# Attention probabilities are split by query rows and turned by DMA; scores run seven units ahead, heads load by fives

## The reference

```python
q = heads(hidden_states @ W_q); k_t = heads(text_ehs @ W_k); v_t = heads(text_ehs @ W_v)
probs_t = softmax(einsum('bhsd,bhtd->bhst', q, k_t) * Dh ** -0.5)
text_out = einsum('bhst,bhtd->bhsd', probs_t, v_t)
attn_scores = einsum('bhsd,bhnd->bhsn', q, heads(ip_ehs @ W_k_ip)) * Dh ** -0.5
qsem = l2norm(einsum('bhst,bte->bhse', probs_t, text_ehs))
sem = einsum('bhse,bne->bhsn', qsem, l2norm(ip_ehs))
probs_ip = softmax(attn_scores + 0.5 * sem) * spatial_mask
out = (text_out + probs_ip @ v_ip) @ W_out + b_out + residual
```

## Time and profile before

| what | us |
|---|---|
| median of three runs | 1904.91 |
| lowest and highest | 1904.19, 1909.89 |
| the profiled execution | 1911.86 |
| its span | 1910.1 |
| PE busy in the span | 1878.8 |
| DVE busy | 1460.1 |
| ACT busy | 1378.5 |
| POOL busy | 907.3 |

### The profile page before, as it was taken

One profiled execution on the slowest core, in us unless ns is written; L12 is line 12 of the kernel. 1 busy time (PEld: TensorE's weight loads), 2 busy tenths in 40 slices (PEclk: granted clock), 3 DMA queues, 4 the chain that ended last, 5 costly groups with the idle time before them and its releaser, 6 DMA issues.

```text
span 1910.1 us, 52608 instructions
## 1 busy us (share of the span) xinstructions
PE 1878.8 (98%) x15701; PEld 1275.4 (67%) x15701; DVE 1460.1 (76%) x3192; ACT 1378.5 (72%) x2644; POOL 907.3 (47%) x1076
## 2 busy tenths in 40 slices
PE   5999999999999999999999999999999999999999
PEld 3776667666666666666666666666666666666555
DVE  5454544788888888888888888888888888888885
ACT  3344554788888888888888888888888888888611
POOL 2121222455555555555555555555555555555421
PEclk8899999999999999999999999999999999999999
DMA  5345555111111111111111111111111111111023
GB/s 174 105 133 130 165 141 140 40 26 27 45 26 27 27 43 26 27 41 29 26 27 45 26 27 27 43 26 27 27 43 27 27 26 44 28 27 51 1 86 107
DMA packets 120643, 102.10 MB, mean 53 GB/s; under 512 B 53369, under 2 KB 114433, under 8 KB 120609
## 3 DMA queue, kind: packets, MB, share of 16 engines
q1 hardware_dynamic: 118304, 99.50, 19.3%
q10 hardware_dynamic: 2304, 2.14, 0.4%
HBM read 67.21 MB, written 34.39 MB: 53 GB/s over the span
## 4 chain that ended last, share of the span: by engine, by line
PE 96%; DVE 2%; ACT 1%; issue 0%; DMA 0%; SPq 0%; ACTq 0%; DVEq 0%
PE bank L1291 29%; PE bank L1292 18%; PE bank L1272 15%; PE bank L1157 13%; PE bank L1265 7%; PE bank L1297 3%; PE bank L1358 3%; PE bank L1290 3%; PE bank L1216 1%; PE bank L1359 1%; DVE reduced L894 1%; DMA reduced<-in_ctx 0%; PE bank L1343 0%; PE bank L1140 0%; ACT u_sb L688 0%
## 5 line engine op out<-in xcount | busy, mean ns | idle before, releaser
L509 POOL TENSOR_TENSOR weight<-probs,half_hi 128x508 f32<-128x508 f32 x640 | 736.1, 1150 | 649.4 <-DVE discard L973 640.1
L1291 PE MATMUL bank<-u_sb,probs_hi 127*128 127x508 f16 x2560 | 943.4, 375 | 0.0
L1292 PE MATMUL bank<-u_sb,probs_hi 127*128 127x508 f16 (+3 forms) x2560 | 760.8, 297 | 0.0
L966 DVE TENSOR_REDUCE neg_max<-bank 128x1 f32<-128x508 f32 x640 | 439.4, 687 | 239.1 <-PE bank L1265 239.1
L712 ACT ACTIVATE probs_hi<-bank 127x512 f16<-127x512 f32 x640 | 382.1, 597 | 234.8 <-PE bank L1272 234.8
L1290 PE MATMUL bank<-v_ring,probs_hi 127*128 127x41 f16 x2560 | 468.5, 183 | 0.0
L978 DVE SCALAR_TENSOR_TENSOR probs_lo<-bank,probs_hi 127x512 f16<-127x512 f32 x640 | 438.8, 686 | 2.4 <-ACT probs_hi L712 2.4
L701 ACT ACTIVATE probs<-bank,neg_max 128x508 f32<-128x508 f32 x640 | 434.3, 679 | 0.5 <-DVE neg_max L966 0.4
L973 DVE SCALAR_TENSOR_TENSOR discard<-bank,weight 128x508 f32<-128x508 f32 x640 | 433.4, 677 | 1.1 <-PE bank L1292 1.1
L708 ACT ACTIVATE half_hi<-probs 128x508 f16<-128x508 f32 x640 | 401.4, 627 | 20.4
L1290 PEld LDWEIGHTS bank<-v_ring,probs_hi 127*128 127x128 f16 x2560 | 248.0, 97 | 226.2 <-issue 0.8
(11 more groups left out here) (160 smaller groups left out, 1340.1 us busy)
## 6 DMA issues: line engine op xcount, KB each, us to landing
x_sb<-in_x SPq DMA_DIRECT2D x16, 640.0 KB, 5.4
reduced<-in_ctx SPq DMA_DIRECT2D x32, 256.0 KB, 5.1
q_ring<-q_parts SPq DMA_DIRECT2D x160, 48.0 KB
k_ring<-k_parts SPq DMA_DIRECT2D x160, 47.6 KB
u_parts<-u_sb SPq DMA_DIRECT2D x8, 825.5 KB, 4.2
u_sb<-u_parts SPq DMA_DIRECT2D x8, 825.5 KB, 4.7
v_parts<-v_sb SPq DMA_DIRECT2D x8, 820.0 KB, 8.0
v_ring<-v_parts SPq DMA_DIRECT2D x160, 41.0 KB
```

The costliest lines, as they stand in the source:

```text
L509: nc.gpsimd.tensor_tensor(weight[:, st % 2, :], probs[:, st, :], half_hi[:, st % 2, :], ALU.subtract)\
L966: nc.vector.tensor_reduce(neg_max[:, st:st + 1], bank[S_BANK + st % 2][:, 0:T], AX.X, ALU.max, negate=True)\
L1291: nc.tensor.matmul(y, hi_k, u_sb[0:TP, par, GH[k]:GH[k] + T], start=(k == 0), stop=False)
L1292: last = nc.tensor.matmul(y[:, k * TP:T], hi_k, u_sb[0:TP, par, UL[k]:UL[k] + U_COLS[k]], start=False, stop=(k == TT - 1))
```

## The change

- The four PE transposes, probs_lo from the bank, half_hi and weight are gone. ACT now shifts the exponential by a constant (an extra instruction on 128 x 1 that makes exp_bias out of neg_max) so that its result is already in the scale of the halves. ACT rounds probs to f16 in query rows (hi, into the tile flat, which lies over the weights' tile wkv). lo is probs minus hi, also in query rows: DVE makes it for 5 units of 8, POOL for units 1, 4 and 6 of 8. POOL adds lo to probs in place (weigh), and the norm takes that sum.
- One DMA transpose on SP turns both halves of two units, 128 x 2048 f16 (turn), into a ring of eight units (turned, over the tile late). flat holds four units.
- The scores have four banks and run seven units ahead (LEAD). probs is a ring of ten.
- Loads come for five heads at once into two buffers (load_group and load_values, seven DMAs). ACT starts them, in step 9 of 20, and the Gram matrix of the next batch but one too.
- The copy of the v bank stands in ACT's even steps j, for the pair that ends with unit j-9 (DRAIN_AT).
- In the first stage all stores are finished before the first loads of the loop are started. The columns of W_q, W_k and W_k_ip come in another order, for which a mask is made by sixteen chained selects at the start, and the image-prompt scores take all 80 columns for each tile.
- Several tiles now lie over others; the image-prompt matrices of the last stage are made earlier.

```diff
@@ sizes, rings and banks
-    RING = 4
...
+    GROUP = 5
+    ROUND = 2 * GROUP * ST
+    ROUNDS = UNITS // ROUND
+    LEAD = 7
+    PROB_RING, FLAT_RING, TURNED_RING = 10, 4, 8
+    POOL_LO = (1, 4, 6)
...
-        S_BANK, PT_BANK, Y_BANK, O_BANK = 0, 2, 4, 6
+        S_BANK, Y_BANK, O_BANK = 0, 4, 6
+        S_BANKS = 4
...
+        def need(eng, signal, count):
+            if not isinstance(count, int) or count > 0:
+                eng.wait_ge(signal, count)
...
+        def load_group(eng, b, i, n):
+            heads = bass.ds(i * GROUP, GROUP)
+            for a0, copies in ((0, 3), (3, 2), (5, 1)):
+                eng.dma_start(q_ring[a0 * D:(a0 + copies) * D, n], q_parts[b, 0:copies, :, heads, :].rearrange("a d h s -> (a d) h s"))\
+                   .then_inc(group_loaded[n], 16)
+            for part, (a0, copies) in enumerate(((0, 3), (3, 2), (5, 1))):
+                eng.dma_start(k_ring[a0 * D:(a0 + copies) * D, n],
+                              k_parts[b, part, :, heads, :].unsqueeze(0).broadcast_to([copies, D, GROUP, T]))\
+                   .then_inc(group_loaded[n], 16)
+        def load_values(eng, b, i, n):
+            eng.dma_start(v_ring[:, n].rearrange("p h k c -> p h (k c)"),
+                          v_parts[b, bass.ds(i * GROUP, GROUP), :, :].rearrange("h p c -> p h c")).then_inc(values_loaded[n], 16)
@@ SyncE
+            def turn(rnd, j):
+                sp.wait_ge(hi_ready, ROUND * rnd + j + 2)
+                apart(sp)
+                lo_made(sp, rnd, j)
+                apart(sp)
+                lo_made(sp, rnd, j + 1)
+                apart(sp)
+                need(sp, unit_done, ROUND * rnd + j + 2 - TURNED_RING)
+                apart(sp)
+                r, f = j % TURNED_RING, j % FLAT_RING
+                sp.dma_start_transpose(turned[:, r:r + 2].rearrange("p r a k s -> p (r a k) s"),
+                                       flat[:, f:f + 2].rearrange("p r a k t -> p (r a k t)")).then_inc(turned_landed[r // 2], 16)
@@ GpSimd
+            for d in range(D):
+                if d:
+                    pool.wait_ge(consts_made, 14 + d)
+                nc.gpsimd.affine_select(out=spreadmask[:, :, :], in_=spreadmask[:, :, :], compare_op=ALU.not_equal, fill=1.0,
+                                        base=-H * d, pattern=[[P, NC], [-1, H]], channel_multiplier=1).then_inc(consts_made, 1)
...
+            pool.wait_ge(scores_filled, 1)
+            nc.gpsimd.memset(flat[:, :, :, :, TP:P], 0.0).then_inc(flat_padded, 1)
+            def remainder(rnd, j):
+                pool.wait_ge(hi_ready, ROUND * rnd + j + 1)
+                rows = flat_rows(j)
+                nc.gpsimd.tensor_tensor(rows[:, 1, :, 0:TP], probs[:, j % PROB_RING, :].rearrange("p (k t) -> p k t", k=TT),
+                                        rows[:, 0, :, 0:TP], ALU.subtract).then_inc(pool_lo_ready, 1)
+            def weigh(rnd, j):
+                lo_made(pool, rnd, j)
+                own = probs[:, at(rnd, j)[1] % PROB_RING, :].rearrange("p (k t) -> p k t", k=TT)
+                nc.gpsimd.tensor_tensor(own, own, flat_rows(j)[:, 1, :, 0:TP], ALU.add).then_inc(weight_ready, 1)
@@ ScalarE
...
+            act.wait_ge(parts_saved, 1 + 16 * 2 * NC * B)
+            act.wait_ge(v_saved, 1 + 16 * B)
+            act.wait_ge(u_saved, 1 + 16 * B)
+            def shift(rnd, j):
+                rnd, j = at(rnd, j)
+                act.wait_ge(row_max_found, ROUND * rnd + j + 1)
+                nc.scalar.activation(exp_bias[:, j % 4:j % 4 + 1], neg_max[:, j % 4:j % 4 + 1], ACT.Copy, bias=LOG_SCALE)\
+                  .then_inc(bias_ready, 1)
+            def exp(rnd, j):
+                act.wait_ge(bias_ready, ROUND * rnd + j + 1)
+                need(act, norms_done, ROUND * rnd + j + 1 - PROB_RING)
+                nc.scalar.activation(probs[:, j % PROB_RING, :], bank[S_BANK + j % S_BANKS][:, 0:T], ACT.Exp,
+                                     bias=exp_bias[:, j % 4:j % 4 + 1]).then_inc(probs_ready, 1)
+            def hi(rnd, j, first):
+                act.wait_ge(probs_ready, ROUND * rnd + j + 1)
+                if not (first and j < FLAT_RING):
+                    landed(act, rnd, j - FLAT_RING)
+                    need(act, weight_ready, ROUND * rnd + j + 1 - FLAT_RING)
+                nc.scalar.activation(flat_rows(j)[:, 0, :, 0:TP], probs[:, j % PROB_RING, :].rearrange("p (k t) -> p k t", k=TT),
+                                     ACT.Copy).then_inc(hi_ready, 1)
             def drain_out(g, pair, slot):
-                act.wait_ge(out_filled, 2 * g + pair + 1)
-                act.wait_ge(head_reduced, g + 1)
+                act.wait_ge(unit_done, ST * g + 2 * pair + 2)
+                need(act, head_reduced, g - 1)
                 nc.scalar.activation(out_raw[:, 2 * slot + pair].rearrange("p u c -> p (u c)"),
                                      bank[O_BANK + pair][:, 0:2 * VCOLS], ACT.Copy).then_inc(out_drained, 1)
...
+            DRAIN_AT = LEAD + 2
+            LOAD_AT = 9
+            def units(rnd, b, half, u_par, first, last):
+                for j in range(ROUND):
+                    if first and j == 0:
+                        shift(0, 0)
+                    exp(rnd, j)
+                    if not (last and j == ROUND - 1):
+                        shift(rnd, j + 1)
+                    hi(rnd, j, first)
+                    if j % 2 == (DRAIN_AT + 1) % 2 and not (first and j < DRAIN_AT + 1):
+                        g, st = (j - DRAIN_AT) // ST, (j - DRAIN_AT) % ST
+                        drain_out(ROUND // ST * rnd + g, st // 2, g % 2)
+                    n = j // (ROUND // 2)
+                    if j % (ROUND // 2) == LOAD_AT and not (first and n == 0) and not (last and n == 1):
+                        free = 1 - n
+                        act.wait_ge(scores_filled, ROUND * rnd + n * ROUND // 2)
+                        act.wait_ge(unit_done, ROUND * rnd + n * ROUND // 2)
+                        nb, i = (b, half * 2 + 1) if n == 0 else (b, 2) if half == 0 else (b + 1, 0)
+                        load_group(act, nb, i, free)
+                        load_values(act, nb, i, free)
@@ VectorE
+            def norm(rnd, j):
+                rnd, j = at(rnd, j)
+                v = ROUND * rnd + j
                 dve.wait_ge(quad_filled, v + 1)
-                dve.wait_ge(weight_ready, 2 + v + 1)
...
+                dve.wait_ge(weight_ready, v + 1)
+                nc.vector.scalar_tensor_tensor(discard[:, j % 2, 0:T], bank[Y_BANK + j % 2][:, 0:T], 1.0, probs[:, j % PROB_RING, :],
+                                               ALU.mult, ALU.mult,
+                                               accum_out=norms[:, bass.ds(v, 1)]).then_inc(norms_done, 1)
+            def lo(rnd, j):
+                rnd, j = at(rnd, j)
+                dve.wait_ge(hi_ready, ROUND * rnd + j + 1)
+                rows = flat_rows(j)
+                nc.vector.tensor_tensor(rows[:, 1, :, 0:TP], probs[:, j % PROB_RING, :].rearrange("p (k t) -> p k t", k=TT),
+                                        rows[:, 0, :, 0:TP], ALU.subtract).then_inc(dve_lo_ready, 1)
+            def units(rnd, first):
+                for j in range(ROUND):
+                    row_maximum(rnd, j)
+                    if not (first and j < LEAD + 1):
+                        norm(rnd, j - LEAD - 1)
+                    if not (first and j == 0) and not by_pool((j - 1) % ROUND):
+                        lo(rnd, j - 1)
@@ TensorE
...
+                        last = nc.tensor.matmul(bank[IPS_JOB[0]][:, s * HIP:(s + 1) * HIP], q_full[0:rn, c, s * P:(s + 1) * P],
+                                                kip_batch[0:rn, c, :], start=(c == 0), stop=(c == NC - 1))
...
+            def scores(rnd, j):
+                rnd, j = at(rnd, j)
+                n, h, st = j // (GROUP * ST), j // ST % GROUP, j % ST
+                if j % (GROUP * ST) == 0:
+                    pe.wait_ge(group_loaded[n], 16 * 6 * (rnd + 1))
+                need(pe, probs_ready, ROUND * rnd + j + 1 - S_BANKS)
+                nc.tensor.matmul(bank[S_BANK + j % S_BANKS][:, 0:T], q_ring[:, n, h, st * P:(st + 1) * P], k_ring[:, n, h, :],
                                  start=True, stop=True).then_inc(scores_filled, 1)
...
+            def unit(rnd, j, par, ahead):
+                n, h, st = j // (GROUP * ST), j // ST % GROUP, j % ST
+                y, o = bank[Y_BANK + st % 2][:, 0:T], bank[O_BANK + st // 2][:, (st % 2) * VCOLS:(st % 2 + 1) * VCOLS]
+                both = turned[0:TP, j % TURNED_RING]
+                if ahead:
+                    scores(rnd, j + LEAD)
+                if j % (GROUP * ST) == 0:
+                    pe.wait_ge(values_loaded[n], 16 * (rnd + 1))
+                landed(pe, rnd, j)
+                need(pe, norms_done, ROUND * rnd + j - 1)
+                if st % 2 == 0:
+                    need(pe, out_drained, ROUND // 2 * rnd + j // 2 - 1)
                 for k in range(TT):
...
```

(5 more changed lines are left out.)

331 lines of the change are left out of this document (131 added, 200 removed).

## The result

The changed kernel takes 2864.11 us (median of 4 runs, 2858.90 to 2872.21), the kernel before beside it 1907.4 us (median of 4 runs, 1904.19 to 1911.77): ratio 1.5017, 95% interval [1.4963, 1.5072]. The forecast was 2615 us, range 2390 to 2870. The direction and the mechanism came as forecast; the size lies at the upper edge, 249 us above the number.

The account below looks back on a forecast made before the run. TensorE alone was taken to bound the kernel at 2.26 us a unit. Drain, second loop, loads, POOL and DVE and clock gave 3.35 over 640 units, plus 14 us outside: 2615 us, range 2390 to 2870.

Parts of the forecast that it names:

- The drain: Attention loop: before every even unit TensorE waits for ACT's bank copy, 2.27 us from newest scores to block, 2.85 a unit.
- The second loop: Attention loop: DVE's lo ahead of the row maximum lengthens the way to 4.46 us, 6.07 a pair, 3.03 a unit.
- The loads: Seven DMA issues per five heads on ACT's stream take 4.4 us, half hidden: +0.15 us a unit (0 to 0.22).
- The transposes themselves cost nothing here: DMA transposes in the loop land in 3.2 us; up to about 6 us is covered and costs nothing.
- POOL and DVE: Loop: a lo on DVE starting under a POOL operation waits for its end: +0.07 us a unit (0 to 0.11).
- The clock: Loop: waiting TensorE gets the lower clock for one in five blocks, one to a pair: +0.14 us a unit.
- Outside the loop: Start +5 us, wider image-prompt scores +4, turn into the loop +15, end -10: together +14 us.
- Rival 1: Loop: clock stays full, loads partly hidden, 3.0 to 3.2 us a unit, median 2391 to 2519 us; chance 0.27.
- 2 (all at 1.2 GHz): Loop: the clock falls and stays at 1.2 GHz, 4.49 us a unit, 3340 us; chance 0.07.
- Rival 3: Loop: the copy is released earlier, so its wait vanishes: 1820 us, or 1648 if POOL is not held up; chance 0.05.
- Rival 4: Loop: slow transposes landing in 9 us add about 1.0 us a unit, 3250 us; chance 0.08.
- what would show it: Profile signs: even units wait about 2 us, scores-to-copy 2.2 to 2.4, pair 5.7 to 6.7, clock 0.8 to 1.0, transposes under 6.

Follow-up runs that it names:

- e11: e10 with loads of one partition each in the loop, most of the data left out: 1793 us.
- e1: The changed kernel with ACT's copy out of the output bank one step earlier, in step u+5 instead of u+6: 2331 us.
- e2: The changed kernel with ACT's copy out of the output bank two steps earlier, in step u+4: 2291 us.
- e3: The changed kernel without the loads of queries, keys and values in the loop, most of the heads' data left out: 2527 us.
- e7: e2 with loads of one partition each, most of the data left out: 2027 us.
- e8: e2 with loads of one partition each and without POOL's addition of the rounded halves: 1900 us, ratio 0.997.
- e10: e2 without POOL's addition, loads on SyncE one behind each of seven transposes, older work no longer queued behind the newest scores, copy in step u+3: 2012 us.
- e12: e10 with all its data, eight slots instead of four for rounded rows, and values kept by partition in DRAM: 1954 us.
- e4: The changed kernel with the same seven load issues per group on ACT, each of one partition, most of the data left out: 2552 us.

## Why the prediction was right, and where its sum was off

**The bound before, and what is removed.** Right: 0.44 us of transposes a unit left TensorE. e11, with almost no waits, has it busy for 1.90 us a unit against 1.82 in the forecast.

**The drain.** Right in mechanism, and shown by e1 and e2: one step earlier takes 533 us away. The string was put at 2.27 us and is 2.04. Three terms were too long: the rounding starts 0.10 behind the shift, not 0.20, the drain 0.52 behind the rounding, not 0.60, and the last hand-over is 0.06 us shorter. The second loop was put at 6.07 us a pair and is 5.78. Waits without loads were put at 1.24 us a unit (2.99 less 1.82, and 0.07 for the read path) and measured 1.00 in e3: 0.24 too high.

**The loads.** This is the step that failed, with the clock below. They were priced by ACT's time alone, "+0.15 a unit (0 if all is covered, 0.22 if none)". Measured 0.52, of which the issues are 0.04. "The transposes themselves cost nothing here" was right for a transpose alone: it lands in 4.3 us, where 3.2 was estimated and up to 6 were free. It was taken for granted that it lands so beside the loads too. The row on the free DMA engines (0.12 busy) spoke of a loop without transposes; with them the share is 0.46 even without loads (e3), and seven loads at once then push a landing to as much as 21.6 us.

**POOL and DVE.** Right in the changed kernel: the residual's mean is 0.82 us against 0.69, 0.13 on five of eight units, 0.08 a unit (forecast 0.07). That POOL is held up too, which no row of before showed, is seen in e2: 2.63 us for two additions, where 2.23 would do. The rule that the prediction weighed (the Trainium skill, SBUF — State Buffer, Practical consequences: the second of the two fully blocks) fits these rows in both directions.

**The clock.** Mis-sized most. One block in five of those in the loop was to run at the lower level, +0.14 a unit. The mean of L1376 is 435 ns in the groups above; single ones (changed kernel, 500 to 1500 us, ns min/median/max):

```profile
L1376 PE MATMUL bank<-u_sb,late x1072: 373/375/595, 502.1 to 1499.5; 127*128 127x508 f16 x179
```

If 375 and 595 are its two levels, 27% of them ran low (60 of 220), nearly three times the one block in ten that the sum took, which is +0.39. By the busy time it is 2.33 less the 1.88 of e11 at full clock: +0.45. How the clock goes with the standing time is seen across the runs: it is 1.00 with no standing, 0.98 to 0.99 with 0.16 to 0.45 us of standing a unit in e7, e8 and e11, 0.89 to 0.94 with 0.38 to 1.04, and 0.84 with 1.39. The length of single waits may matter beside their sum: e10 and e12 stand less than e7, in waits of up to 7.5 us for a transpose where e7's longest for DVE's norm is 3.1, and are granted less (0.93 against 0.98). No run changed the clock alone, so this is an order seen in fourteen kernels and not a cause shown.

**The sum by terms, us a unit.**

```
                               forecast   measured
TensorE's own work              1.82       1.88   e11, its 1.90 less 1% of clock
clock, without the loads        0.14       0.32   e3 busy 2.20 less 1.88
standing, without the loads     1.24       1.00   e3
loads, standing and clock       0.15       0.52   3.72 less 3.20
                                3.35       3.72
```

The 0.37 us are 237 us in 640 units. That the standing time of 1.39 us came out exactly (1.24 + 0.15) is luck: 0.24 too much on the drain and 0.24 too little on the loads. The time is 6 us below the upper end of the range: with the drain sized right and the range as wide, that end would be 154 us lower, 2716, and 2864 outside it.

**Outside the loop.** TensorE and DVE started behind POOL at 9.24; TensorE's first transposes now start at 15.37, +6 (forecast +5). The wider image-prompt scores cost nothing that is seen: 275 ns at the median (row below) against 276 in the earlier trace rows, and the last u store is issued at 339.76 against 340.72, so the rest of the first stage took the 6 us back. The turn into the loop was put at +15 and is +32 measured from that store: the block starts at 375.37. Line 1307 and timeline of the changed kernel:

```profile
L1307 PE MATMUL bank<-reduced,work x192: 232/275/443, 70.1 to 331.4; 128*128 128x80 f32 x128, 64*128 64x80 f32 x64
...
15.37 0.90 PE L1258 MATMUL bank<-ident,x_sb 128*128 128x128 f32 x3 [15.37 <-POOL spreadmask L503]
...
339.76 0.34 SPq L404 DMA_DIRECT2D u_parts<-u_sb  x1
...
354.76 4.38 SPq L429 DMA_DIRECT2D u_sb<-u_parts  x2
...
373.34 0.60 PE L1357 MATMUL bank<-x_sb,work 96*128 96x508 bf16 x1 [7.94 <-DMA u_sb<-u_parts]
...
375.37 0.20 PE L1375 MATMUL bank<-v_ring,late 127*128 127x41 f16 x1 [1.42 <-DMA late<-wkv]
```

The sixteen issues end at 359 us, where 355 was put, and the last ones land late behind the others: TensorE waits for u until 373, where 360 was forecast (the u loads take 12.7 us to landing, not 4.7). It is the same mistake as with the transposes, a landing time read from a quiet row.

**The rivals.** Rival 1 (full clock) and 2 (all at 1.2 GHz) are both out: 0.84 lies between. Rival 3's reading of the order is out; its price was wrong as well, since e2 makes exactly its edit and takes 2.85 us a unit, not 2.09. Rival 4 had a landing of 9 us for all transposes; what came is that landing, and longer, for a few beside each load. Of "what would show it", three lines failed: transposes don't all land in under 6 us "with nobody waiting for them" (up to 21.6), the pitch of a pair is 7.4 us on average and not 5.7 to 6.7, and scores-to-copy reads 2.04 where the residual is not in the way, below 2.2.

## What to carry to other kernels

Where an engine's program puts an old buffer's release behind work on the newest input, more buffers don't shorten the wait (argued from the order; no run here adds score banks); moving the release by one step was worth 533 us here. A transfer that runs all through a loop must be priced together with what else moves in that loop: landing times read from a quiet row, and busy shares read from a loop without it, both mislead. And an engine that is made to wait may be granted less clock: here that was 0.45 of the 3.72 us a unit, and the sum had 0.14 for it.

## What the runs showed of the hardware

- A DMA transpose of 128 x 2048 f16 within SBUF lands in 4.2 to 4.3 us without loads beside it (e3, at most 6.1) and holds SP's queue for 1.8 us at the median (e3). It keeps the 16 DMA engines busy for 2.9 us, 1.43 for each unit (e3). Beside 58 KB of loads a unit its packets take 1.92 us a unit (changed kernel), and the work of transposes and loads together is 0.6 to 0.9 us above that of the runs without the loads' bytes; in the kernel before the loop's loads made 0.27.
- Seven loads of 1.16 MB in all, issued within 4.5 us, stretch a transpose to as much as 21.6 us (changed kernel); the same loads issued one by one behind transposes on SP leave at most 12.7 (e10).
- An f32 addition on POOL and a two-input residual on DVE hold up each other: on DVE 0.69 becomes 1.42 us at the median of e2; on POOL the mean goes from 1.12 (e4) to 1.23 us (e2), and two additions that one residual meets take 2.63 in place of 2.23.
- f32 matmuls with 80 moving columns take as long as those with 32 or 16: 275 against 276 ns at the median, though the shortest went from 192 to 232 (kernel before, changed kernel).
